# Expert tiles of 256 rows with stationary weights, copied per tile by DMA, in a transformer block with mixture of experts

## The reference, cut to what matters

```
x = layernorm(x + attention(x))
h = x + layernorm(x, g1, b1) @ attn_w.T
t = layernorm(h, g2, b2)                       # 4096 tokens x 128
top_vals, top_idx = top_k(t @ gate_w.T, 2);  rw = softmax(top_vals)
for e in range(8):
    g = t @ gate_proj[e].T;  u = t @ up_proj[e].T         # tokens x 512
    out += weight_of_token_for_e * ((silu(g) * u) @ down_proj[e].T)
x = layernorm(x + (h + out))
```

## Time and profile before

| | us |
|---|---|
| median of 3 runs | 406.17 (405.88 to 406.26) |
| span of the profiled execution | 403.7 |
| outside the span, median less span | 2.5 |
| first expert load issued | 150.3 |
| PE in the experts stage, first gate matmul to last down matmul | 157.58 to 361.57 |
| first load of `finish` issued | 364.86 |

### The profile page before, as it was taken

The page is one execution under the profiler, slowest core; times in us unless marked ns, Lnnn a source line. Parts: engine busy times, 40 slices in busy tenths (PEclk is TensorE's granted clock), DMA queues, the critical chain, the costliest instruction groups (busy, mean ns, idle before and its releaser), DMA issues.

```text
span 403.7 us, 9351 instructions
## 1 busy us (share of the span) xinstructions
PE 309.9 (77%) x2041; PEld 268.2 (66%) x2042; DVE 287.6 (71%) x1108; ACT 189.6 (47%) x474; POOL 210.4 (52%) x276
## 2 busy tenths in 40 slices
PE   3999888888765204999999999999999999970000
PEld 2788777776544103888888898988888898860000
DVE  2589999999998725766666666666666666634992
ACT  3887757677643202444444434344443434420552
POOL 0031888788787785243434343444434444354992
PEclk9999999999975555999999999999999999995555
DMA  6610111144511131112111111111111111105871
GB/s 200 198 52 26 42 63 57 54 145 151 198 35 41 47 94 25 41 39 56 42 52 39 52 41 45 50 40 52 39 52 41 45 50 39 42 12 156 213 205 53
DMA packets 33853, 29.52 MB, mean 73 GB/s; under 512 B 4753, under 2 KB 31381, under 8 KB 33696
## 3 DMA queue, kind: packets, MB, share of 16 engines
q1 hardware_dynamic: 24576, 18.36, 16.3%
q0 software_dynamic: 4320, 8.47, 6.1%
q10 hardware_dynamic: 4928, 2.36, 2.0%
HBM read 18.02 MB, written 11.61 MB: 73 GB/s over the span
## 4 chain that ended last, share of the span: by engine, by line
PE 54%; DVE 29%; issue 7%; DMA 4%; POOL 3%; ACT 2%; SPq 0%; DVEq 0%; ACTq 0%; POOLq 0%
PE bank L503 15%; PE bank L465 8%; PE bank L467 8%; PE bank L466 8%; PE bank L493 8%; DVE y L715 2%; DVE rows L673 2%; PE bank L476 2%; DVE x_all L873 2%; POOL expert_rows L913 2%; DVE n L658 2%; DVE st L754 1%; DVE st L721 1%; DVE topi L780 1%; DVE w_lo L769 1%
## 5 line engine op out<-in xcount | busy, mean ns | idle before, releaser
L963 POOL DMA_INDIRECT moe_rows<-ysb,idx x71 | 71.3, 1005 | 35.6 <-issue 18.5
L503 PE MATMUL bank<-wd,hidT 128*128 x568 | 75.4, 276 | 0.7 <-ACT ysb L608 0.6
L913 POOL DMA_INDIRECT expert_rows<-rows,place x64 | 63.4, 990 | 17.9 <-issue 13.9
L859 DVE SCALAR_TENSOR_TENSOR hid<-sg,xrow,bank 128x512 f32<-128x512 f32 x71 | 53.1, 748 | 24.2 <-PE bank L467 22.5
L503 PEld LDWEIGHTS bank<-wd,hidT 128*128 128x128 f32 x568 | 69.0, 192 | 1.4 <-issue 1.3
L608 ACT ACTIVATE ysb<-bank 128x128 f32<-128x128 f32 x71 | 19.8, 278 | 102.6 <-PE bank L503 102.6
L465 PE MATMUL bank<-w_hi,t_hi 128*128 x142 | 62.2, 438 | 3.8 <-DVE t_lo L851 3.8
L959 POOL TENSOR_TENSOR idx<-xrow,zero_i 128x1 int32<-128x1 int32 x71 | 12.7, 180 | 86.9 <-issue 56.9
L849 DVE CAST t_hi<-t 128x128 fp32r<-128x128 f32 x71 | 19.9, 281 | 51.8 <-ACT t L595 51.8
L467 PE MATMUL bank<-w_hi,t_lo 128*128 x142 | 56.5, 398 | 0.0
L466 PE MATMUL bank<-w_lo,t_hi 128*128 x142 | 56.2, 396 | 0.0
(11 more groups left out here) (122 smaller groups left out, 592.7 us busy)
## 6 DMA issues: line engine op xcount, KB each, us to landing
xrow<-expert_rows SPq DMA_DIRECT2D x71, 65.0 KB, 1.8
w_raw<-weights SPq DMA_DIRECT2D x16, 256.0 KB, 3.9
yin<-moe_rows SPq DMA_DIRECT2D x16, 256.0 KB, 3.8
xin<-x SPq DMA_DIRECT2D x16, 128.0 KB, 2.2
wd<-weights SPq DMA_DIRECT2D x1, 2048.0 KB, 9.2
out<-x_all ACTq DMA_DIRECT2D x16, 128.0 KB, 3.3
moe_rows<-ysb,idx POOLq DMA_INDIRECT x71, 2.4
expert_rows<-rows,place POOLq DMA_INDIRECT x64, 2.3
```

Source lines behind the costliest of these rows:

```text
L503: last = mm(banks[7][:, 0:P], hidT[i2][:, c * P:(c + 1) * P], wd[:, bass.ds(w + c * P, P)], start=(c == 0), stop=(c == NC - 1))
L859: V.scalar_tensor_tensor(hid[i2][:, :], sg[i2][:, :], xrow[r1][:, D:D + 1], banks[2 + i2][:, :], ALU.mult, ALU.mult).then_inc(sm["hid_done ...
L913: G.indirect_dma_start(out=expert_rows[:, :], out_offset=bass.IndirectOffsetOnAxis(ap=place[b % NR][:, t, k:k + 1], axis=0), in_=rows[b % ...
L963: G.indirect_dma_start(out=moe_rows[:, :], out_offset=bass.IndirectOffsetOnAxis(ap=idx[r3][:, :], axis=0), in_=ysb[r3][:, :], in_offset=No ...
```

## The change

Tiles of the experts stage have 256 rows: 8192 / 256 + 7 = 39 tiles. The two projections swap operands. A 128x128 block of weights is now the stationary operand and the 256 token columns (`t_hi`, `t_lo`, 128 x 256) the moving one, so the result comes out with the inner dimension on the partitions. The product of silu and up is then already the `hidT` that the down product wants, and the transposes of `hid` (L493) and their copy (L866) go away. The stationary weights are taken from `w_now`, two buffers of 1 MB; SP fills one per tile with two DMAs of 512 KB (128 partitions x 4 KB) from the resident array `w_split`, once the tile before last has ended its up matmuls. Gate and up run in two halves of 256 inner columns, with the transposes of the next tile and the down product of the tile before between the halves. The mixing weight is now applied by ACT when it copies the down result. Each tile has two scatters. The arrays of the front and of the experts stage share one arena, since `w_now` takes room. The fill rows behind each expert's region are 256 instead of 128. In a step ACT now does the silu of half 0, `t32` of the next tile, `ysb` of the tile before and the silu of half 1; DVE does the product of half 0, `t_hi` and `t_lo` of the next tile and the product of half 1. The diff, cut, shows the sizes and then SP, PE, ACT, DVE and GpSimd in this order.

```diff
-REGION = T + P
+HALVES = 2
+PT = HALVES * P
+REGION = T + PT
-MOE_TILES = T * TOPK // P + E - 1
+MOE_TILES = T * TOPK // PT + E - 1
+W_EXPERT = 2 * 2 * INTER
+W_HALF = W_EXPERT // HALVES
...
+        w_split = sb("w_split", [P, E, HALVES, 2, 2, INTER // HALVES], F32R)
+        w_now = ring("w_now", [P, HALVES, 2, 2, INTER // HALVES], F32R)
...
             def load_rows(s, r, live):
                 if live(0):
                     if far(s, RING):
-                        sp.wait_ge(sm["hid_done"], s - (RING - 1))
+                        sp.wait_ge(sm["ysb_done"], s - (RING - 1))
                         sp.wait_ge(sm["idx_done"], s - (RING - 1))
...
+                    sp.dma_start(xrow[r][:, :, :], rows_at(at)).then_inc(xr_in[r], 16)
+                    w = sp.value_load(eoff[0:1, bass.ds(s, 1)], min_val=0, max_val=(E - 1) * W_EXPERT)
+                    if far(s, 2):
+                        sp.wait_ge(sm["u_ps"], HALVES * (s - 2) + HALVES)
+                    for h in range(HALVES):
+                        sp.dma_start(w_now[r % 2][:, h, :, :, :].rearrange("p l j n -> p (l j n)").bitcast(F32),
+                                     w_flat[:, bass.ds(w + h * W_HALF, W_HALF)]).then_inc(wn_in[h][r % 2], 16)
...
-            def gate_up(w, j, bank, i2):
-
-                mm(bank[:, :], t_hi[i2][:, :], w_hi[:, j, w], start=True, stop=False)
-                mm(bank[:, :], t_hi[i2][:, :], w_lo[:, j, w], start=False, stop=False)
-                return mm(bank[:, :], t_lo[i2][:, :], w_hi[:, j, w], start=False, stop=True)
+            def gate_up(n, i2, h):
+
+                for j in range(2):
+                    for c in range(2):
+                        bank = banks[2 * h + j][:, c * PT:(c + 1) * PT]
+                        at = slice(c * P, (c + 1) * P)
+                        mm(bank, w_now[i2][:, h, 0, j, at], t_hi[i2][:, :], start=True, stop=False)
+                        mm(bank, w_now[i2][:, h, 1, j, at], t_hi[i2][:, :], start=False, stop=False)
+                        last = mm(bank, w_now[i2][:, h, 0, j, at], t_lo[i2][:, :], start=False, stop=True)
+                    last.then_inc(sm["g_ps" if j == 0 else "u_ps"], 1)
 
             def experts(s, r, live):
...
+                    pe.wait_ge(sm["tlo_done"], i + 1)
+                    pe.wait_ge(wn_in[0][i2], turn(i, i2, 2))
+                    if far(i, 1):
+                        pe.wait_ge(sm["hT_sb"], HALVES * (i - 1) + 1)
+                    gate_up(i, i2, 0)
                 if live(0):
...
+                    for h in range(HALVES):
+                        last = nc.tensor.transpose(banks[6][:, h * P:(h + 1) * P], xrow[r][:, h, 0:D], ident)
+                    last.then_inc(sm["xr_ps"], 1)
                 if live(2):
...
-                    for c in range(NC):
-                        last = nc.tensor.transpose(banks[4 + i2][:, c * P:(c + 1) * P],
-                                                   hid[i2][:, c * P:(c + 1) * P], ident)
-                    last.then_inc(sm["hT_ps"], 1)
...
+                    pe.wait_ge(sm["hT_sb"], HALVES * i + HALVES)
                     if far(i, 1):
                         pe.wait_ge(sm["ysb_done"], i)
...
+                    for h in range(HALVES):
+                        for c in range(NC):
+                            last = mm(banks[7][:, h * D:(h + 1) * D], hidT[i2][:, c, h * P:(h + 1) * P],
+                                      wd[:, bass.ds(w + c * P, P)], start=(c == 0), stop=(c == NC - 1))
                     last.then_inc(sm["y_ps"], 1)
+                if live(1):
+                    i, i2 = s - 1, (r - 1) % 2
+                    pe.wait_ge(wn_in[1][i2], turn(i, i2, 2))
+                    if far(i, 1):
+                        pe.wait_ge(sm["hT_sb"], HALVES * (i - 1) + 2)
+                    gate_up(i, i2, 1)
...
+            def silu(s, r, h):
+                i, i2 = s - 1, (r - 1) % 2
+                act.wait_ge(sm["g_ps"], HALVES * i + h + 1)
+                if far(i, 1):
+                    act.wait_ge(sm["hT_sb"], HALVES * (i - 1) + h + 1)
+                A(sg[h][:, :], banks[2 * h][:, :], ACT.Silu).then_inc(sm["sg_done"], 1)
...
+                    for h in range(HALVES):
+                        last = A(ysb[r2][:, h, :], banks[7][:, h * D:(h + 1) * D], ACT.Identity,
+                                 scale=xrow[r2][:, h, D:D + 1])
...
+            def product(s, r, h):
...
+                V.tensor_tensor(hidT[i2][:, 2 * h:2 * h + 2, :].rearrange("p c t -> p (c t)"), sg[h][:, :],
+                                banks[2 * h + 1][:, :], ALU.mult).then_inc(sm["hT_sb"], 1)
...
+                    for h in range(HALVES):
+                        G.indirect_dma_start(
+                            out=moe_rows[:, :], out_offset=bass.IndirectOffsetOnAxis(ap=idx[r2][:, h:h + 1], axis=0),
+                            in_=ysb[r2][:, h, :], in_offset=None, bounds_check=last_row, oob_is_err=False
+                        ).then_inc(y_sent[r2], 16)
```

More of the change, by code:

```diff
@@ L178, in block_kernel @@
         fill_at = sb("fill_at", [1, E], I32)
-        fill = sb("fill", [P, ROW])
+        fill = sb("fill", [P, HALVES, ROW])
         NW = E * INTER
         WP = NW // B
-        w_raw = ring("w_raw", [P, 2, WP], n=NWR)
-        w_hi = sb("w_hi", [P, 2, NW], F32R)
-        w_lo = sb("w_lo", [P, 2, NW], F32R)
+        w_raw = [view(2 * WP).rearrange("p (j n) -> p j n", j=2) for _ in range(NWR)]
+        space[0] = 0
+        w_split = sb("w_split", [P, E, HALVES, 2, 2, INTER // HALVES], F32R)
+        w_now = ring("w_now", [P, HALVES, 2, 2, INTER // HALVES], F32R)
         wd = sb("wd", [P, NW])
[L187 to L193, removed]
+        xrow = ring("xrow", [P, HALVES, ROW], n=RING)
+        t32 = ring("t32", [P, PT])
+        t_hi = ring("t_hi", [P, PT], F32R)
+        t_lo = ring("t_lo", [P, PT], F32R)
+        sg = [view(512) for _ in range(2)]
+        hidT = [view(NC * PT).rearrange("p (c t) -> p c t", c=NC) for _ in range(2)]
         warm = sb("warm", [P, 1])
         zero_i = sb("zero_i", [P, 1], I32)
-        idx = ring("idx", [P, 1], I32, n=RING)
-        ysb = ring("ysb", [P, D], n=RING)
-        yin = ring("yin", [P, NT, TOPK, D], n=RING)
+        idx = ring("idx", [P, HALVES], I32, n=RING)
+        ysb = [view(HALVES * D).rearrange("p (h d) -> p h d", h=HALVES) for _ in range(RING)]
+        yin = [view(NT * TOPK * D).rearrange("p (t k d) -> p t k d", t=NT, k=TOPK) for _ in range(RING)]
         st3 = sb("st3", [P, NT, 6])
@@ L237, in block_kernel, with rows_at @@
         xr_in, y_sent, y_in, o_sent = sems("xr_in", RING), sems("y_sent", RING), sems("y_in", RING), sems("o_sent", RING)
+        wn_in = [sems(f"wn_in{h}_") for h in range(HALVES)]
         block = ctx.enter_context(nc.Block())
+        def rows_at(at):
+            return expert_rows[bass.ds(at, PT), :].rearrange("(p h) d -> p h d", h=HALVES)
         def straight_steps(step, n_items, depth):
@@ L838, in _ @@
             dve.wait_ge(sm["ereg_done"], 1)
-            V.scalar_tensor_tensor(ereg[:, :], row_f[:, :], float(P), ereg[:, :], ALU.mult, ALU.add
+            V.scalar_tensor_tensor(ereg[:, :], row_f[:, :], float(PT), ereg[:, :], ALU.mult, ALU.add
                                    ).then_inc(sm["ereg_done"], 1)
@@ L853, in experts @@
                 if live(1):
[L854 to L857, removed]
-                        dve.wait_ge(sm["hT_ps"], i - 1)
-                    V.scalar_tensor_tensor(hid[i2][:, :], sg[i2][:, :], xrow[r1][:, D:D + 1], banks[2 + i2][:, :],
-                                           ALU.mult, ALU.mult).then_inc(sm["hid_done"], 1)
-                if live(2):
-                    i, i2 = s - 2, r % 2
-                    dve.wait_ge(sm["hT_ps"], i + 1)
-                    if far(i, 2):
-                        dve.wait_ge(sm["y_ps"], i - 1)
-                    V.tensor_copy(hidT[i2][:, :], banks[4 + i2][:, :]).then_inc(sm["hT_sb"], 1)
-            looped_steps(dve, experts, MOE_TILES, 3)
+                    product(s, r, 1)
+            looped_steps(dve, experts, MOE_TILES, 2)
             def finish(s, live):
```

140 lines of the change are left out of this document (65 added, 75 removed).

## The result

The changed kernel took 419.89 us, median of 4 runs (415.58 to 427.32), beside 406.22 for the kernel before on the same chip. The forecast was 396.7, with 388 to 415 as its range. A second measurement gave 419.48 (417.36 to 425.81) beside 405.62. Some runs of the changed kernel (two of the first four, one of the second four) took over 1.5% longer than its fastest, and they are left out of the ratios, which are 1.0255 (95% interval 1.0225 to 1.0286) and 1.0323 (1.0275 to 1.0371). The profile shown here is that of the second measurement; the profiled execution took 418.63, with a span of 416.8.

What follows compares the result with a forecast made beforehand. PE alone bounds the experts stage; 39 steps of 4.88 us make 190.3, its end comes 11.3 us earlier, an extra copy and scatter add 1.8: 406.2 - 9.5 = 396.7 us, range 388 to 415.

Steps and rivals of the forecast that it cites:

- T: PE's step per 256-row tile in the experts stage: 24x + 2.00 = 4.88 us, with matmul pitch x at 0.12.
- The rule of the Trainium skill: Rival on gate and up: weight loads overlap matmuls only across different row groups, so all stand alone; 502 us, chance 0.04.
- The copies: Part on SP's DMAs per step: weight halves and rows land before PE needs them, with R taken as 377 GB/s.
- 2.25 + 1.049 / R = 5.03: Landing of `xrow` in us after SP's wait ends: fixed costs and row data, plus 1.049 MB of weights; due at 6.32.
- The clock: Sign of being wrong: any row in the experts stage at clock 0.5, which would double the matmul part.
- The copies are the bound: Rival in the experts stage: SBUF to SBUF weight copies set the step; 461 us at 188 GB/s, chance 0.17.
- R below 243: Copy rate in GB/s at which the gain is gone: T = 5.12 us, 1.049 / R = 4.31.
- 225 GB/s: Milder case of the copies rival in the experts stage: T = 5.47 us, 420 us in all.
- At 188: Copy rate if both SBUF ends share 377 GB/s: engines need 6.5 us per step, +64, 461 us.
- A handoff per step: Rival in the experts step: DVE or ACT delivers late; 413 us at T = 5.3, chance 0.07.
- the two that I had named: DVE's product of the second half, or ACT's copies before its second silu, over 0.6 us later than predicted.
- the mild cases of both: Mild copies and handoff in the experts stage, over which the 8 in 10 range reaches up: 388 to 415.

Runs made afterwards that it cites:

- kernel with small copies: The changed kernel, but from the fifth tile on each half of the weights is refilled with 128 B per partition instead of 4 KB: 397.29 us.
- kernel with half buffers: Changed kernel with rows loaded a tile earlier, PE's register load at step start, and each weight half refilled after its own up matmuls: 395.18 us.
- bodies of 4 and 16: The changed kernel with 4 or 16 steps in the experts loop body instead of 8: 410.62 us with 4, 428.03 us with 16.
- two kernels with half buffers: The kernel with half buffers with 8 steps in the loop body, 395.18 us, and the same with 16 steps, 394.99 us.

## Why the prediction was wrong

**What held.** The pitch of a 256-column matmul with its own weight load is (246.01 - 241.15 - 0.22 - 1.79) / 24 = 0.119, where I took 0.12; T without waits is 4.86, where I had 4.88. So the weight loads stay hidden. The rule of the Trainium skill, "TensorE: Matmul & The Clock Gate", Part 3, as the prediction reads it, would have put a step at 7.6; the trace disagrees with it at 0.119. The copies ran at 381 to 414 GB/s where the windows are full, at the 377 that I took or above. ACT's copy with a scale took 364 ns (0.28 to 0.45), DVE's last product cost 0.92 (1.0). The kernel with small copies, in which nothing else of the change is undone, measured 397.3. Some of that closeness is luck: in the kernel with half buffers, whose last down product ends at 349.33, the first gate matmul starts 1.9 us earlier than predicted (156.00 for 157.9), and TensorE's clock stays at half until 161.9, which costs 3.0 where 1.3 was put.

**What failed** is the part "The copies", in the sum 2.25 + 1.049 / R = 5.03 and "1.3 us early". Its rate was right; its landing was 6.98 after the wait. In two calm steps the wait ends at 235.34 and 240.19 and the rows land at 240.90 and 245.57, that is 5.6 and 5.4 after it (5.03 was put), and 0.44 and 1.15 before PE is ready for them. A fetch takes more than that. Three things were not in the sum.

- SP's queue. I gave 0.2 us from the wait to the first copy and nothing between the issues. Behind the wait stand two issues, 1.16 us, the address arithmetic, and the register load, in all 2.68 before `xrow` is issued. The steps without a fetch have this too, and their rows are in time. The step said "behind this wait stands the load of `xrow`", and priced its bytes only. The register load has a row in the trace of before, 0.267 us, but its threefold length beside copies has none there.
- The fetch of instructions, which runs 0.94 us on one engine and goes with landings some 1.4 us later (4.1 to 4.3 after the issue, for 2.5 to 2.9). It turned "nearly late" into late in 8 steps of 39. It was in the trace of before too (three between 150 and 345), where nothing hung on it.
- PE's register load. In the handoffs I counted what DVE and ACT give to the down product, and not what PE itself does between its waits. The wait for `xrow`, once it is not free, holds back the `value_load` behind it, and the down product starts 0.6 to 1.1 us late a second time. It does so even where the rows are nearly on time: the chain has 5.38 us for the step from 241.50 (0.26 of "issue", and a down product of 2.05 where one that follows at once takes 1.79), and 4.86 for the next.

Where the time is, from the first gate matmul to the last down product: 156.34 to 370.53 here, 214.2 us, and 156.00 to 347.29, 191.3, in the kernel with half buffers, a difference of 22.9. The waits of PE are 8.1 + 5.4. The chain has 2.05 for a down product that could not follow at once and 1.79 for one that could; counted from the end of the matmul before, 24 down products lost up to 0.26 in this way, 5.2 us together, and eight pairs of transposes 0.22 each, 1.8. And after two late steps the granted clock fell:

```profile
330.00:331.00 1.00, 1.00 (x7) 1.00 (x6) 0.00 (x0) 0.00 (x0) 0.00 (x0) 0.50 0.82 248
331.00:332.00 1.00, 1.00 (x7) 1.00 (x7) 0.00 (x0) 0.00 (x0) 0.00 (x0) 0.50 0.05 17
332.00:333.00 1.00, 1.00 (x6) 1.00 (x6) 0.00 (x0) 0.00 (x0) 0.00 (x0) 0.50 0.00 0
```

PE starts 6 or 7 matmuls a us here, where the full clock has 10 or 11 (198 to 201, above): some 3.4 us at 1.2 GHz, 1.7 lost, twice, 3.4. At the start of the stage it is the other way round: the clock is full from 159.2 here and from 161.9 in the kernel with half buffers, which gives 1.5 back. The sum is 22.4 of 22.9. The clock was named in the prediction as what would prove it wrong, without a price.

That PE's waits come from SP's order and its own, each experiment with an edit of order shows. That fetches make the rows late is shown by their count and place, and by the bodies of 4 and 16. That a fetch holds back the rows' part on its own engine is inferred: the trace does not name the engine. Why the exposed register load shows in every other calm step can be read off the landings: the down product starts at the earliest 1.1 us after the rows land (240.90 and 241.98), which leaves a gap where they are 0.44 us early, as there, and none where they are 1.15 early, as in the next step. Not shown is what slows a register load beside copies: the kernel with small copies shows that they do.

**The rivals.** "The copies are the bound" had the right place and a wrong mechanism: its sign was R below 243, and the full microseconds above have 381 or more. Its 420 us, for 225 GB/s, is the nearest number to the 419.5 measured, and that is luck: nothing ran at 225. Its sums were uneven too. At 188 it counts the row load and the scatter on the engines, 0.95 us of a step, and at 225 and 243 it does not; with them the step at 225 is 5.61 (425 us) and the gain is gone at 251. "A handoff per step", 413 us at 0.07, had the kind of loss right, a wait of PE's own in many steps; the handoff was none of the two that I had named. The one was dismissed on a rate and the other on the time that an engine is busy, and what decided is work that the profile counts as no engine's: issue, register, fetch. The range ended at 415 since the mild cases of both were small; it left out a load that misses by 0.3 to 0.9 us and pays twice.

## What to carry to other kernels

When a transfer is queued behind a wait, price everything in that queue between the end of the wait and its issue, register loads as well as issues, and look in the same way at what stands behind the consumer's wait in the consumer's own program. Issue small urgent loads ahead of large ones, read registers before the first wait of a step, and release a double buffer by halves. If the slack is under the 1.4 us or so that a fetch cost a landing here, count on an instruction fetch to use it.

## What the hardware showed that I had not expected

- A register load from SBUF takes 0.27 us on SP and 0.30 on PE; beside copies its median is 0.85 on SP, and 0.91 (of 39, from 0.30 to 0.95) on PE when it stands at the start of the step. Not each one is slow: PE's at 202.13 took 0.31, with the DMA engines 0.88 busy from 202 to 203.
- In the microseconds that SBUF to SBUF copies in rows of 4 KB fill, the DMA engines move 381 to 414 GB/s. The copies cost the matmuls beside them nothing that shows (PE busy for 180.00 of 180 us, steps of 4.86 us, as in the kernel with small copies).
- A fetch of instructions takes 16 KB through one of the DMA engines, 0.94 us here. The eight row loads in whose time one ran landed 4.1 to 4.3 us after their issue, the calm ones 2.5 to 2.9.
- A down product of 16 matmuls takes 2.05 us in the chain when it follows idle time, and 1.79 when it does not. The two transposes take 0.44 and 0.22.
- The granted clock fell to 1.2 GHz after the late steps at 328 and 358 (idle 1.7 us each time), and not after the one at 202 (1.5 us) or that at 346 (1.8 us). What decides between them these runs don't tell. Nor do they tell whether it is what spreads the changed kernel's runs, where the two kernels with half buffers, which have no such stretch, spread by 0.6 and 0.1.
